# Attention stage of a graph network kernel: running sums of all tiles in SBUF, unpadded product rows, weights summed on VectorE, q staged by TensorE, index copies and bias on VectorE

## The reference

```python
q = (nfeat @ Wq.T).reshape(n, HEADS, HEAD_DIM) / SCALING      # 8 heads of 32
k = (nfeat @ Wk.T).reshape(n, HEADS, HEAD_DIM)
v = (nfeat @ Wv.T).reshape(n, HEADS, HEAD_DIM)
attn = jnp.einsum('ehd,ehd->eh', k[src], q[dst]) + attn_bias
m = jax.ops.segment_max(attn, dst, num_segments=n)
a = jnp.exp(attn - m[dst])
s = jax.ops.segment_sum(a, dst, num_segments=n)
out = jax.ops.segment_sum(v[src] * (a / s[dst])[:, :, None], dst, num_segments=n)
```

## Time and profile before

| | |
|---|---|
| three runs, median | 4279.67 us |
| the three runs | 4279.67, 4288.94, 4276.35 us |
| span of the profiled execution | 4287.7 us |
| busy in the span: PE, DVE, ACT, POOL | 2980.3, 2479.7, 1089.2, 2064.3 us |
| attention loop, 220.45 to 1596.8 us | 1376.35 us |
| busy in it: PE, DVE, ACT, POOL | 678.0, 1026.3, 219.0, 882.5 us |
| phases behind it, 1596.8 to 4287.7 us | 2690.9 us |

### The profile page before, as it was taken

One profiled execution on the slowest core, in us unless ns is written; L12 is line 12 of the kernel. 1 busy time (PEld: TensorE's weight loads), 2 busy tenths in 40 slices (PEclk: granted clock), 3 DMA queues, 4 the chain that ended last, 5 costly groups with the idle time before them and its releaser, 6 DMA issues. The chain is left out here.

```text
span 4287.7 us, 49015 instructions
## 1 busy us (share of the span) xinstructions
PE 2980.3 (70%) x13743; PEld 2189.0 (51%) x13743; DVE 2479.7 (58%) x4593; ACT 1089.2 (25%) x2192; POOL 2064.3 (48%) x1781
## 2 busy tenths in 40 slices
PE   4335545544455545485688867999979897899798
PEld 2211211111111114364588856777758886688686
DVE  8457777777777764443699964111125666534443
ACT  1111111111111112121155542333334554100221
POOL 4666666666666642544387318888820000001233
PEclk7666776776766766698799987999989998999899
DMA  2466666666666647444266647456532443355433
GB/s 96 149 184 192 196 197 189 195 191 190 193 193 193 192 135 253 135 68 91 60 230 170 159 186 110 13 13 13 6 44 88 139 132 121 132 181 175 124 65 53
DMA packets 317791, 583.65 MB, mean 136 GB/s; under 512 B 100508, under 2 KB 221600, under 8 KB 308736
## 3 DMA queue, kind: packets, MB, share of 16 engines
q0 software_dynamic: 160880, 294.23, 31.7%
q1 hardware_dynamic: 137552, 235.63, 16.9%
q10 hardware_dynamic: 19264, 52.66, 3.9%
HBM read 421.02 MB, written 163.96 MB: 136 GB/s over the span
## 5 line engine op out<-in xcount | busy, mean ns | idle before, releaser
L2157 PE MATMUL gnn_p_msg<-gnn_msg,gnn_ident 128*128 128x512 f32 x928 | 678.0, 898 | 766.6 <-issue 458.0
L2110 POOL DMA_INDIRECT gnn_got<-kv,gnn_index x928 | 882.5, 951 | 455.5 <-issue 290.4
L2157 PEld LDWEIGHTS gnn_p_msg<-gnn_msg,gnn_ident 128*128 128x128 f32 x928 | 260.1, 294 | 1183.8 <-issue 1156.2
L2231 DVE TENSOR_TENSOR gnn_prod<-gnn_got,gnn_p_both 128x2048 f32<-128x2048 f32 x116 | 265.4, 2288 | 232.5 <-issue 190.2
L2537 POOL DMA_INDIRECT weight_table<-cell_of,cell_at x192 | 316.9, 1651 | 94.2 <-issue 50.0
L2537 POOL DMA_INDIRECT count_table<-cell_of,cell_at x192 | 315.0, 1641 | 68.0 <-issue 55.5
L2703 PE MATMUL tables_p_pair<-tables_spread,tables_hot 128*128 128x100 f32 x2816 | 335.4, 278 | 17.0 <-DVE tables_spread L2677 12.1
L2703 PEld LDWEIGHTS tables_p_pair<-tables_spread,tables_hot 128*128 128x128 f32 x2816 | 323.4, 193 | 28.7 <-DVE tables_spread L2677 20.3
L799 DVE SCALAR_TENSOR_TENSOR ffn_acc<-ffn_pC,ffn_gates,ffn_acc 128x256 f32<-128x256 f32 x200 | 88.9, 480 | 394.4 <-PE ffn_pC L643 384.5
L2245 DVE TENSOR_TENSOR gnn_msg<-gnn_got,gnn_p_both 128x2048 f32<-128x2048 f32 x116 | 264.7, 2282 | 72.8 <-ACT gnn_p_both L2138 40.2
L2964 PE MATMUL gnn_p_sum<-gnn_hs,gnn_edge 128*128 x2500 | 286.6, 277 | 15.4 <-DVE gnn_edge L2993 15.0
(11 more groups left out here) (445 smaller groups left out, 4703.0 us busy)
## 6 DMA issues: line engine op xcount, KB each, us to landing
slabs<-weight_table SPq DMA_DIRECT2D x25, 1600.0 KB
weight_table<-tables_weight_slab SPq DMA_DIRECT2D x11, 3200.0 KB
count_table<-tables_count_row SPq DMA_DIRECT2D x11, 3200.0 KB
gnn_cell<-count_table ACTq DMA_DIRECT2D x50, 576.0 KB
state<-gnn_out SPq DMA_DIRECT2D x116, 136.0 KB
ffn_xs<-by_expert SPq DMA_DIRECT2D x60, 260.0 KB, 3.3
gnn_got<-kv,gnn_index POOLq DMA_INDIRECT x928
gnn_cell<-count_table ACTq DMA_DIRECT2D x25, 448.0 KB
```

The costliest lines, as they stand in the source:

```text
L2110: pool.indirect_dma_start(out=got[k][:, r, :], out_offset=None, in_=kv_dram, in_offset=rows_at(index[k][:, r:r + 1])).then_inc(gathered[k] ...
L2157: last = nc.tensor.matmul(p_msg[k][:], ident[:], msg[k][:, r:r + 2].rearrange("p r h d -> p (r h d)"), start=(r == 0), stop=(r == R - 2))
L2231: dve.tensor_tensor(prod[v][:, :, :, 0:HD], keys, over(p_q[v], wide, "p (a h d) -> p a h d", a=1, h=HEADS), ALU.mult)
```

## The change

Running sums, sum of weights and maximum of all 25 tiles (and a spare one) now lie in SBUF (`acc`), cleared at the start by DVE and faded and added to in place; SP stores each tile once, when its last body is done (`done_at`). Rows of `prod` have 32 elements and there is one `prod`. The bias is added by DVE behind the reduction. DVE copies the maximum in and the indices out, which takes four register loads a body on DVE (tile of this body and of the late one, place of this body and of the one four ahead). PE stages q by a product with the scaled identity, two bodies ahead. The weighted values are written over the gathered values, PE sums them by eight products of 256 columns, and POOL waits for that sum (`summed[k]`) where it waited for DVE's product. The sum of weights is taken by DVE from the PSUM weights of the same body. ACT is left with two exponentials. The diff, cut:

```diff
+        acc = s.sb("acc", [P, TILES + 1, STATE])
+                for t in range(TILES):
+                    finished = sp.value_load(done_at[0:1, t:t + 1], min_val=1, max_val=TILES * MAIN + LAG)
+                    sp.wait_ge(out_ready, finished)
+                    sp.dma_start(state_dram[t * P:(t + 1) * P, :], acc[:, t, :]).then_inc(stored, 16)
...
                         wait_apart(index_ready, g * SETS + (k + 1))
-                        wait_apart(released[k], g + 1)
+                        wait_apart(summed[k], g + 1)
...
                         act.wait_ge(shifted, b + 1)
-                        act.activation(p_weight[v], score[v][:, 0:R, :].rearrange("p r h -> p (r h)"),
+                        act.activation(p_weight[v][:, 0:R * HEADS], score[v][:, 0:R, :].rearrange("p r h -> p (r h)"),
                                        ACT.Exp).then_inc(weights_ready, 1)
-                        act.activation(score[1 - v][:, R, :], peak[k], ACT.Identity, bias=first[:, bass.ds(b + 1, 1)])
-                        act.activation(keep[k][:], score[v][:, R, :], ACT.Exp)
-                        act.activation(weight[k][:], score[v][:, 0:R, :], ACT.Exp).then_inc(keep_ready, 1)
-                        stage(b + 1, 1 - v)
-                        find_index(b + SETS, k)
+                        act.activation(keep[k][:], score[v][:, R, :], ACT.Exp).then_inc(keep_ready, 1)
...
+                def stage(b, v):
+                    rows_of = q[:, bass.ds(piece(pe, b) // MAIN, 1), :].rearrange("p a d -> p (a d)")
+                    nc.tensor.matmul(p_q[v][:, 0:F], scaled[:], rows_of, start=True, stop=True).then_inc(staged, 1)
...
-                        for r in range(0, R, 2):
-                            last = nc.tensor.matmul(p_msg[k][:], ident[:],
-                                                    msg[k][:, r:r + 2].rearrange("p r h d -> p (r h d)"),
-                                                    start=(r == 0), stop=(r == R - 2))
-                        last.then_inc(summed, 1)
+                        pe.wait_ge(msg_ready, b + 1)
+                        stage(b + 2, v)
+                        for r in range(R):
+                            last = nc.tensor.matmul(p_msg[k][:, 0:F], ident[:], got[k][:, r, F:2 * F],
+                                                    start=(r == 0), stop=(r == R - 1))
+                        last.then_inc(summed[k], 1)
...
+                def find_index(b, k):
+                    dve.tensor_copy(index[k][:], source[:, bass.ds(piece(dve, b) * R, R), 0]).then_inc(index_ready, 1)
+                def tile_at(b):
+                    return dve.value_load(tile_of[0:1, bass.ds(b, 1)], min_val=0, max_val=TILES)
...
+                        dve.tensor_tensor(prod[:], keys, over(p_q[v][:, 0:F], [P, R, HEADS, HD], "p (a h d) -> p a h d", a=1, h=HEADS),
+                                          ALU.mult)
+                        t, late = tile_at(b + LAG), tile_at(b)
+                        at = piece(dve, b)
+                        dve.tensor_copy(score[v][:, R, :], peak_of(t))
+                        find_index(b + SETS, k)
                         dve.drain()
                         dve.tensor_reduce(score[v][:, 0:R, :].rearrange("p r h -> p (r h)"),
-                                          prod[v][:].rearrange("p r h d -> p (r h) d"), AX.X, ALU.add)
+                                          prod[:].rearrange("p r h d -> p (r h) d"), AX.X, ALU.add)
+                        dve.drain()
+                        dve.tensor_tensor(score[v][:, 0:R, :], score[v][:, 0:R, :], bias[:, bass.ds(at * R, R), 1:EDGE], ALU.add)
...
+                        fade(late, k - LAG)
+                        dve.drain()
                         dve.wait_ge(weights_ready, b + 1)
-                        dve.tensor_tensor(msg[k][:], values,
+                        dve.tensor_tensor(values, values,
...
+                        dve.tensor_reduce(weight_sum[k][:], p_weight[v][:, 0:R * HEADS].rearrange("p (r h) -> p h r", h=HEADS),
+                                          AX.X, ALU.add)
+                        add_sums(late, k - LAG, g + (2 if k >= LAG else 1))
```

More of the change, by code:

```diff
@@ new lines, in _ @@
+                        dve.tensor_reduce(weight_sum[k][:], p_weight[v][:, 0:R * HEADS].rearrange("p (r h) -> p h r", h=HEADS),
+                                          AX.X, ALU.add)
+                        add_sums(late, k - LAG, g + (2 if k >= LAG else 1))
+                total = group_count(dve) * SETS
+                for end in range(LAG):
+                    late = tile_at(total + end)
+                    dve.drain()
+                    dve.wait_ge(keep_ready, total)
+                    fade(late, end - LAG)
+                    dve.drain()
+                    add_sums(late, end - LAG, group_count(dve) + 1)
```

129 lines of the change are left out of this document (48 added, 81 removed).

## The result

The changed kernel takes 4313.58 us (median of four runs, 4309.33 to 4330.86), the kernel before 4278.62 on the same chip (four runs, 4276.35 to 4288.94). The ratio is 1.008, with a 95% interval of 1.0058 to 1.0102: longer by 0.8%, where 4116 was forecast. Executions of one kernel on one chip lie up to 1% apart (the ten of experiment 18), so the difference is small but clear of noise. The profiled execution spans 4312.7 us against 4287.7.

What follows compares the result with a forecast made beforehand. It took the attention loop to be held by ACT's slow sequencer at 11.70 us a body; DVE would then bind at 10.3, 116 bodies making 1194.8 us, -162.3, with the end -164: 4279.67 to 4116 us, range 4080 to 4270.

Steps and rivals of the forecast that it cites:

- What bounds the kernel now: Attention loop: a ring of waits held by ACT's slow sequencer, 11.70 us a body, 1.67 above POOL's floor of 10.03.
- that DVE is spared I can: Attention loop: the slow register instructions of 0.70 us on ACT and SP don't strike DVE, whose own take 46 ns.
- Rival 4: Slow sequencer moves to engines now looping with register loads; DVE's some 43 instructions at 0.70, 30 us a body, about 6400; 4%.
- ACT leaves the ring: ACT in the loop: 3 of some 20 instructions a body left, 2.1 to 4.2 us, so it waits only for DVE's subtraction.
- SP: SP's stores: 25 instead of 116, waited for by no one in the loop; worth nothing while DVE is the later.
- DVE's body: DVE in the loop: added and saved pieces sum to +0.68, 10.16 us a body, 10.3 with the jump, narrowly the bound.
- Loads under the product: DVE's four register loads a body, 2.4 us, run under the 2.29 us product; the reduction starts at 3.05, +0.69.
- rival 2: DVE's register loads don't run under the product: body 12.6 us, loop 1462, time 4383; 15%.
- Rival 3: DVE's short two-input instructions and copies block POOL's gather issue: 11.4 us a body, time 4245; 12%.
- Rival 1: DVE's additions hide and POOL is the bound at 10.03 us a body: time 4086; 15%.
- Index copies and the buffer's release: POOL's inputs: index written some 25 us early; gather buffer freed by PE after 27 of 40 us, hidden by 13.
- Nine of half the width are about 4: PE's nine 256-column products a body take about 4 us, against 6.74 for the last eight 512-column products before.

Runs made afterwards that it cites:

- experiment 18: Changed kernel without the bounds checks of the loop's register loads, the loads kept: 4284.97 us (ten runs), ratio 1.001 to the kernel before.
- 2: Changed kernel with index, bias and accumulator at fixed or counter-given places, and DVE's four register loads a body kept but their values unused: 4322.10 us.
- 4: Changed kernel gathering q's 1 KB rows in place of 2 KB key and value rows, as many gathers, half the bytes: 4322.14 us.
- 17: Changed kernel run again unaltered on another chip: 4310.65 us against 4278.28 for the kernel before, ratio 1.0078.
- 1: Changed kernel without DVE's four register loads a body, places fixed or from the loop counter: 4291.58 us against 4300.44 for the kernel before, ratio 0.9982.
- 3: Changed kernel without DVE's register loads, plus 24 register additions a body that the compiler dropped: 4290.45 us.
- 5: Changed kernel without register loads on DVE and without PE's one load a body: 4272.75 us against 4292.28 for the kernel before.
- 9: Changed kernel with 4 of a body's 8 gathers left in the loop, the rest gathered once ahead: 4163.43 us against 4298.91 for the kernel before.
- 8: Changed kernel without DVE's register loads, weighted values in their own buffer so POOL needn't wait for PE, q staged by ACT: 4467.87 us.
- 10: Changed kernel with 6 of a body's 8 gathers left in the loop, the rest gathered once ahead: 4166.34 us against 4298.91 for the kernel before.
- 12: Changed kernel with all 8 gathers, and a POOL memset of 640 elements and a drain ahead of each body's gathers: 4516.21 us, ratio 1.0497.
- 6: Kernel before with ACT's two register loads a body taken away, places fixed: 4293.82 us against 4292.28, ratio 0.9992.
- 13: Changed kernel without DVE's register loads, plus 24 semaphore increments a body on DVE: 4082.0 us, on a chip where the kernel before takes 4064.9.
- 13 to 16: 13, then three runs on its chip with POOL waiting for landed gathers: changed kernel each body, every second body, kernel before each body: 4300.38, 4265.13, 4308.46 us.
- 7: Changed kernel without DVE's register loads, weighted values in their own buffer so POOL needn't wait for PE, q still staged by PE: 4399.52 us.

## Why the prediction was wrong

*What bounds the kernel now.* Right in what it read: the loop was held by ACT's slow sequencer. The step that failed is its last sentence, "that DVE is spared I can". Fast register instructions on DVE in the earlier trace rows were read as a property of DVE. They were the property of an engine whose loop had no register loads and some 310 register instructions in all, where it now has 2500: with loads DVE is struck (result, 2, 4, 17, 18), without them it is not (1, 3, 5, and the kernel before). Whether the loads count or the number isn't shown. In the result DVE's slow sequencer makes up the whole distance to the forecast, 181 us of 186.

*Rival 4* named the mechanism, at 4 in 100, and sized it wrongly: 0.70 us on every DVE instruction, 30 us a body. It strikes some 165 of 2500 and 84 drains, and the body is 11.9. The row that could have sized it was there: on ACT the median load was 282 ns, so most were fast. The loop before had 37 bodies of 15.7 among 78 of 9.85 while ACT bound it. Given to DVE with the same share and excess, that is (78 x 10.3 + 37 x (10.3 + 5.81)) / 115 = 12.2 a body and a time near 4333: an estimate made afterwards, slower, and much nearer to the 11.90 measured than 10.3.

*ACT leaves the ring*: right. It is busy for 77 us, and no wait of DVE for it stands in the view. *SP*: right, nobody waits.

*DVE's body*, 10.16 and 10.3 with the jump: right to 0.1. Measured 10.22 in the result, 10.30 and 10.34 in 9. That is in part luck: the reduction starts 3.3 to 3.4 us after the product instead of 3.05, and the other pieces give it back. *Loads under the product*: right, the score copy is at 2.2 to 2.3 us, and rival 2 is out. *Rival 3* is out by the gathers' 949 ns. *Rival 1* is out: the undisturbed body is 10.3, not 10.03.

*Index copies and the buffer's release*: the indices are in time (5 waits, 1.5 us). POOL does wait for PE's sums, 187.5 us, but with DVE at 11.90 a body this costs nothing in the result. It is a second fault that the first one hides: the sum had PE's work in it but not the lateness of its signal, 3.5 us and up to 20 already in the kernel before, which nobody in POOL's ring waited for then. With DVE fast again (1) that lateness holds the body at 11.63, so the 10.3 would not have come even if DVE had been spared.

*"Nine of half the width are about 4"*: wrong. The 6.74 us of the earlier trace rows are eight entries, four products of 512 columns, and eight of 256 are as many columns: 5.99 us at the end (4.75 in the body at 905.81). The end came to 7.95 us behind the last body, not 6.

*The first two bodies*, not in the sum: 20.8 and 21.9 us. Of the 186 us between the forecast loop (1194.8) and the measured (1380.9) they hold 22, and the other 114 bodies 164.

What the runs showed in place of the failed step: relief of one engine is passed on. ACT and SP (before), DVE (after), PE (1, 5, 8): each takes over the slow instructions or the late signals until POOL stops, and where it pauses in each body no slow stretch comes (9, 10, 12). So four designs with different work on each engine, 1, 5, 6 and the result, lie within 1.3% of each other in their ratios to the kernel before, at 11.5 to 12.1 a body.

Open are: what the 0.70 us is (no DMA queue but the gathers' and the stores' is busy in the loop's slow stretches, the queues named instruction move five packets in the whole loop, and halving the bytes does nothing); why DVE escapes without loads and PE does not; and whether it needs the profiler's recording, as no run here is without it.

The traces give a reason to suspect the recording. The 928 gathers signal 14,848 landings. On the chip of 13 the traces of 13 to 16 hold every one of them. The result's trace holds 4447 (30%), that of the kernel before 2402 (16%), and the traces of the kernels with a pause in each body hold 59% (12), 60% (10) and 79% (9) of theirs. In the result 74% are kept in the first 4 us of a run of gathers and 13% from 16 us on, so records are lost over the same stretch in which DVE turns slow. Halving the bytes in 4 left the number of these events as it was. Records that are lost and sequencers that are held up may have one cause, or the recording may be the cause; no run separates them, and then part of the difference between the chips would be one of recording. The lateness of PE's signals, too, is known only from those that were kept.

Also open is what the changed kernel takes on the chip of 13. Two estimates for that: the kernel before there, if POOL's 10.03 bounds it, and 0.27 a body more, 4065 + 116 x 0.27 = 4096; or run 13 and 0.24 a body more, 4082 + 116 x 0.24 = 4110. Both are slower, by 0.8 to 1.1%.

## What to carry to other kernels

When an engine is slow for a reason that you can't read, price the case in which the slowness follows the work: take the share of slow bodies now and give it to the engine that will bind next. Before a buffer's release is moved to another engine, read how late that engine's signals already are, not how long its work takes. Idle time of an engine that runs ahead, as POOL's here, is no loss until the engine behind it waits. And before many kernels are compared, find out whether the chips differ: here the same kernel takes 4065 us on one and 4278 to 4300 on four others, in executions that were all recorded.

## What was not expected of the hardware

- While POOL issued indirect gathers back to back, one or more sequencers went to steps of 0.70 us an instruction (mostly 689 to 729 ns, twice that at times) until it stopped: DVE a median of 15.5 us after the start of a run, ACT of 20. Behind the first two bodies, with a pause of 3 us in every 10 there was no such stretch (5 and 8 lone instructions of 0.51 to 0.66 us in 10 and 9), with 2.1 us there were a few (50 instructions of 2500). All of it was seen with the profiler recording, which lost up to 84% of the landing events meanwhile.
- On one chip none of it appeared in 1166 us of gathers with 4.2 us of waits in total.
- PE's semaphore signals came up to 20 us behind the modelled end of the matmul (22 in 5), and up to 52 and 47 in 7 and 8; DVE's and ACT's stayed at 0.01 us.
- On POOL the next gather started 3.06 us after a memset of 0.65 us ended, a drain between them, so the pause of 12 could not be made shorter in this way.
- The bounds checks of four register loads cost 0.86 us a body (10.22 to 9.36), although the loads themselves lie under a product.
